# A transformer block with attention to a context and routed experts: another order for the cross stage, and element 0's cross queries split and sent by GpSimd

## The reference

```python
xn = ada_ln(x, t_emb, ...)                      # layer norm, scale and shift from the condition
x = x + mha(xn, xn, xn, sa ...)                 # self attention: 16 heads of 8, 512 keys
x = x + mha(x, u, u, ca ...)                    # cross attention to the 77 context rows
xn = ada_ln(x, t_emb, ln2 ...)
x = x + gelu(xn @ ffn_w1 + b1) @ ffn_w2 + b2    # 128 -> 512 -> 128
# second layer
nx = layer_norm(x)
evidence = softmax(nx @ Wq @ (ctx @ Wk).T * 128**-0.5) @ (ctx @ Wv)
combined = [nx, evidence, condition]            # 384 wide
router_probs = softmax(combined @ router_W + router_b)            # 3 experts
routed = sum_e(expert_e(combined) * router_probs[e])              # silu MLPs, 384 -> 256 -> 128
g = sigmoid(silu(combined @ gate_w1 + b) @ gate_w2 + b)
out = x + g * (routed @ out_w + out_b)
```

## Time and profile before

| | |
|---|---|
| median of 3 runs | 282.58 us (280.73 to 287.5) |
| the profiled execution | 281.71 us, span 279.9 us |
| mean granted TensorE clock | 0.933 |
| busy: TensorE, VectorE, ScalarE, GpSimd | 230.6, 160.4, 156.4, 48.1 us |
| self attention, from first score to last | about 40 to 149 us |
| cross attention of both elements, with the first feed-forward | about 149 to 213 us |
| the rest | about 213 to 280 us |

### The profile page before, as it was taken

The page is one execution under the profiler, slowest core; times in us unless marked ns, Lnnn a source line. Parts: engine busy times, 40 slices in busy tenths (PEclk is TensorE's granted clock), DMA queues, the critical chain, the costliest instruction groups (busy, mean ns, idle before and its releaser), DMA issues.

```text
span 279.9 us, 3963 instructions
## 1 busy us (share of the span) xinstructions
PE 230.6 (82%) x1304; PEld 98.9 (35%) x1304; DVE 160.4 (57%) x377; ACT 156.4 (56%) x280; POOL 48.1 (17%) x124
## 2 busy tenths in 40 slices
PE   3489799896989888789887878659968999968982
PEld 2123243351224222222332214323224555553752
DVE  6979755776588895979630135760035481353543
...
PEclk9999955998699999799999978995999999999999
...
GB/s 237 402 116 219 36 134 128 10 122 99 35 3 1 4 0 3 148 79 2 5 6 4 0 0 2 2 2 5 1 0 1 2 1 0 0 2 37 0 0 37
DMA packets 7012, 13.20 MB, mean 47 GB/s; under 512 B 1746, under 2 KB 5394, under 8 KB 6578
## 3 DMA queue, kind: packets, MB, share of 16 engines
...
## 4 chain that ended last, share of the span: by engine, by line
PE 62%; DVE 17%; ACT 8%; issue 4%; DMA 3%; POOL 3%; SPq 1%; DVEq 0%; POOLq 0%; ACTq 0%
PE UP L755 8%; PE S L703 7%; DVE negm L1214 5%; PE ST L729 4%; PE ST L959 3%; PE S L910 3%; ACT PT L1041 3%; PE UP L758 3%; PE ST L954 2%; ACT mT L1084 2%; PE MB L860 2%; PE ST L978 2%; DMA xn<-x_nat 2%; PE ST L732 2%; PE S L915 1%
## 5 line engine op out<-in xcount | busy, mean ns | idle before, releaser
L1041 ACT ACTIVATE PT<-ST 128x512 f32<-128x512 f32 (+1 forms) x160 | 84.2, 592 | 21.1 <-PE ST L729 13.8
L1214 DVE TENSOR_REDUCE negm<-S 128x1 f32<-128x512 f32 x128 | 80.0, 682 | 27.5 <-PE S L703 27.2
L729 PE MATMUL ST<-QS,KS 51*128 51x512 bf16 x128 | 42.2, 412 | 5.6 <-ACT PT L1041 5.3
L703 PE MATMUL S<-KS,QS 48*128 48x512 bf16 x128 | 42.0, 418 | 3.2 <-DVE negm L1214 2.3
L755 PE MATMUL UP<-PT,VS 128*32 128x512 f32 x256 | 37.3, 657 | 0.0
L703 PEld LDWEIGHTS S<-KS,QS 48*128 48x128 bf16 x128 | 10.1, 97 | 36.8 <-issue 33.7
L577 POOL CAST mpart<-negm 128x16 bf16<-128x16 f32 x16 | 3.2, 199 | 113.6 <-DVE negm L1214 71.6
L1084 ACT COPY mT<-MB 12x512 bf16<-12x512 bf16 x16 | 9.2, 573 | 16.6 <-PE MB L860 16.6
L1218 DVE TENSOR_REDUCE negm<-S 128x4 f32<-128x308 f32 x32 | 13.5, 471 | 5.7 <-PE S L709 5.7
L729 PEld LDWEIGHTS ST<-QS,KS 51*128 51x128 bf16 x128 | 10.7, 96 | 15.0 <-issue 10.7
L624 POOL TENSOR_TENSOR rstd<-rstd,half 128x4 f32<-128x4 f32 x4 | 4.1, 1018 | 55.0 <-DVE rstd L1266 55.0
...
## 6 DMA issues: line engine op xcount, KB each, us to landing
...
```

What stands on the lines that cost most here:

```text
L703: last = mm(S[:, n % 3, :], QS[r, b, 2 * g + jj, i * P:(i + 1) * P], KS[r, b, 2 * g + jj, :], start=True, stop=True)
L729: mm(ST[:, k % 3, :], KS[r, b, block, kt * P:(kt + 1) * P], QS[r, b, block, :], start=True, stop=True).then_inc(s["st_ready"], 1)
L1041: a(PT[0:rows, n % 2, j, :], ST[0:rows, k % 3, :], ACT.Exp, scale=SCALE).then_inc(s["exp_out"], 1)
L1214: v.tensor_reduce(negm[:, slot, e // 4, e % 2, e // 2 % 2:e // 2 % 2 + 1], S[:, n % 3, :], AX.X, ALU.max, negate=True).then_inc(s["max_out ...
```

## The change

The list of steps is reordered in four places, and the resources follow.

- Start: `early_q` stands ahead of the first `mrows`. In each round with `mrows` one `maxima` now comes between `values` and `mrows`. `small_router` moves from round 5 to round 7, `strips_x` from 7 to 8.
- After self attention: `turn`, `project`, `residual`, `queries` stand earlier in the rounds. For element 0 ScalarE writes the cross queries once in fp32 (`rest`), GpSimd makes the three parts, and issues `stack` and, four rounds later as a step `strips_q`, `strips`; before, SP issued them and VectorE made two of the parts. Element 1 keeps ScalarE and VectorE.
- Cross stage: written out in full. All blocks go through ring S; ScalarE copies blocks 3, 5 and 7, VectorE the others. Scores and exponentials of element 1 begin before the last maxima; element 0's norm runs beside them; all exponentials of element 1 come before the first gelu of element 0.
- Tail: the norm and the feed-forward of element 1 stand earlier, among the context attention of element 0. The first norms use UP, MB and S[2]; some banks of the experts change places.

```diff
@@ -145,6 +146,7 @@
             steps.append(fill.pop(0))
     maxima(2)
     maxima(2)
+    steps.append(later.pop(0))
     steps.append(("mrows",) + units[0])
     for n in range(LEAD - 2):
...
     put(3, 0, ("strips1",))
-    for n, step in ((3, "small_ln"), (4, "small_hidden"), (5, "small_router")):
+    for n, step in ((3, "small_ln"), (4, "small_hidden"), (7, "small_router")):
         put(n, len(ROUND) - 1, (step,))
-    put(7, 0, ("strips_x",))
+    put(8, 0, ("strips_x",))
     for n in range(3):
         put(11 + n, len(ROUND) - 1, ("fold", n))
     for n, (unit, kt) in enumerate(rounds):
...
         if unit == (CROSS, 1, 0):
-
-            steps.append(("values",) + rounds[n - 1] + (n - 1,))
-            chain = [step for where in sorted(due) for step in due[where] if step[0] != "reach"]
-            due.clear()
-            gather, natural, normalise, turn, project, residual = chain
-
-            def group_maxima():
-
...
-            put(n + 2, 0, ("norm", 1, 0))
-            put(n + 3, len(ROUND) - 1, ("norm_back", 1, 0))
+            break
         if kind == SELF and kt == 2 and units[at + 1][0] == SELF:
-            put(n, WITH_V + 1, ("mrows",) + units[at + 1])
+            put(n, WITH_V + 2, ("mrows",) + units[at + 1])
         if unit == (SELF, 1, GROUPS - 1):
-            put(n, WITH_V + 1, ("mrows", CROSS, 0, kt))
+            put(n, WITH_V + 2, ("mrows", CROSS, 0, kt))
         if last and g % 2 == 1:
             r = g // 2
             put(n + 1, WITH_V + 1, ("gather", kind, b, r))
-            put(n + 2, 0, ("natural", kind, b, r))
-            put(n + 2, 1, ("normalise", kind, b, r))
+            put(n + 2, 0 if kind == SELF else WITH_V + 1, ("natural", kind, b, r))
+            put(n + 2, 1 if kind == SELF else WITH_V + 2, ("normalise", kind, b, r))
             if r == 1:
-                put(n + 2, WITH_V + 2, ("turn", kind, b))
-                put(n + 3, WITH_V - 1, ("project", kind, b))
-                put(n + 3, WITH_V, ("residual", kind, b))
-                if kind == SELF:
-                    put(n + 3, len(ROUND) - 1, ("queries", b))
-                    put(n + 4, 1, ("rests", b))
-                    put(n + 5, len(ROUND) - 1, ("reach", (3 + b) * GROUPS))
+                put(n + 2, WITH_V, ("turn", kind, b))
+                put(n + 2, len(ROUND) - 1, ("project", kind, b))
+                put(n + 2, len(ROUND) - 1, ("residual", kind, b))
+                put(n + 3, WITH_V - 1, ("queries", b))
+                put(n + 3, WITH_V + 1, ("rests", b))
+                if b == 0:
+                    put(n + 7, len(ROUND) - 1, ("strips_q",))
+                    put(n + 5, len(ROUND) - 1, ("reach", 3 * GROUPS))
+                else:
+                    put(n + 4, WITH_V, ("xblock", 0))
+                    put(n + 4, WITH_V, ("xblock", 1))
         for place, token in enumerate(ROUND):
             for step in due.pop((n, place), []):
...
+            elif token != "V":
                 steps.append(("scores", unit, kt, n, token))
                 steps.append(("exps", unit, kt, n, token))
-    steps += [("values",) + rounds[-1] + (len(rounds) - 1,), ("gather", CROSS, 1, 1)]
...
+    def cross_maxima(g):
+
+        for _ in range(EVENTS[CROSS]):
+            maxima(len(units))
+
+    def attend(n, *js):
+
+        for j in js:
+            steps.append(("scores", rounds[n][0], 0, n, j))
+            steps.append(("exps", rounds[n][0], 0, n, j))
+
+    def values(n):
+        steps.append(("values",) + rounds[n] + (n,))
+
+    n = len(rounds) - GROUPS
+    cross_maxima(0)
+    steps += [("xblock", 2), ("xblock", 3), ("mrows", CROSS, 1, 0)]
+    values(n - 1)
+    steps += [("gather", CROSS, 0, 1)]
+    cross_maxima(1)
+    steps += [("xblock", 4), ("natural", CROSS, 0, 1), ("normalise", CROSS, 0, 1), ("xblock", 5), ("mrows", CROSS, 1, 1)]
+    cross_maxima(2)
+    steps += [("turn", CROSS, 0), ("xblock", 6), ("xblock", 7)]
+    attend(n, 0, 1, 2)
+    steps += [("mrows", CROSS, 1, 2), ("project", CROSS, 0), ("residual", CROSS, 0)]
+    cross_maxima(3)
+    attend(n, 3)
+    steps += [("norm", 0, 0)]
+    attend(n + 1, 0, 1, 2)
+    steps += [("mrows", CROSS, 1, 3)]
+    attend(n + 1, 3)
+    values(n)
+    attend(n + 2, 0, 1, 2)
+    values(n + 1)
+    steps += [("gather", CROSS, 1, 0), ("norm_back", 0, 0)]
+    attend(n + 2, 3)
+    attend(n + 3, 0, 1, 2)
+    steps += [("natural", CROSS, 1, 0), ("normalise", CROSS, 1, 0)]
+    attend(n + 3, 3)
+    steps += [("ffn1", 0, 0), ("ffn1", 0, 1)]
+    values(n + 2)
+    steps += [("ffn1", 0, 2)]
+    values(n + 3)
+    steps += [("gather", CROSS, 1, 1), ("ffn1", 0, 3), ("natural", CROSS, 1, 1), ("normalise", CROSS, 1, 1)]
+    steps += [("ffn2", 0, 0), ("ffn2", 0, 1)]
+    steps += [("ffn2", 0, 2), ("ffn2", 0, 3), ("turn", CROSS, 1), ("norm", 1, 0), ("project", CROSS, 1), ("residual", CROSS, 1)]
+    steps += [("norm", 0, 1), ("norm_back", 1, 0), ("context", 0), ("hidden_x", 0, 0), ("norm_back", 0, 1), ("hidden_x", 0, 1)]
+    steps += [("ffn1", 1, 0), ("context_probs", 0), ("ffn1", 1, 1), ("ffn1", 1, 2), ("context_value", 0), ("ffn1", 1, 3)]
     steps += [("hidden_ev", 0, 0), ("router", 0), ("hidden_ev", 0, 1)]
-    steps += hidden(0, 2, 3)
-    steps += [("norm_back", 0, 1), ("router_probs", 0)]
-    steps += hidden(0, 3, 4) + [("gate", 0)]
-    steps += [("ffn1", 1, c) for c in range(NF)]
...
-    steps += [("ffn2", 1, c) for c in range(NF)]
-    steps += hidden(0, 5, 6) + [("tanh", 0), ("norm", 1, 1)] + hidden(0, 6, 7)
-    steps += [("expert", 0, 1), ("norm_back", 1, 1), ("expert", 0, 2), ("context", 1), ("out", 0)]
-    steps += [("hidden_x", 1, c) for c in range(3)] + [("context_probs", 1)]
-    steps += [("hidden_x", 1, 3), ("context_value", 1), ("hidden_x", 1, 4), ("hidden_x", 1, 5)]
+    steps += hidden(0, 2, 3) + [("ffn2", 1, c) for c in range(NF)] + [("router_probs", 0)]
+    steps += hidden(0, 3, 4) + [("norm", 1, 1), ("gate", 0)]
+    steps += hidden(0, 4, 5) + [("expert", 0, 0)] + hidden(0, 5, 6) + [("norm_back", 1, 1), ("tanh", 0)]
+    steps += hidden(0, 6, 7) + [("context", 1), ("expert", 0, 1), ("hidden_x", 1, 0), ("context_probs", 1)]
+    steps += [("expert", 0, 2), ("out", 0), ("hidden_x", 1, 1), ("context_value", 1)]
+    steps += [("hidden_x", 1, c) for c in range(2, 5)]
     steps += [("hidden_ev", 1, 0), ("router", 1), ("hidden_ev", 1, 1), ("hidden_ev", 1, 2), ("router_probs", 1)]
-    steps += [("gate", 1), ("hidden_ev", 1, 3), ("expert", 1, 0), ("hidden_ev", 1, 4), ("tanh", 1), ("hidden_x", 1, 6)]
+    steps += [("gate", 1), ("hidden_ev", 1, 3), ("expert", 1, 0), ("hidden_x", 1, 5), ("hidden_ev", 1, 4), ("tanh", 1), ("hidden_x", 1, 6)]
     steps += [("hidden_ev", 1, 5), ("expert", 1, 1), ("hidden_ev", 1, 6), ("expert", 1, 2), ("out", 1)]
...
-            return S[:, i, :] if (site, b) == (1, 0) else bank(b, i)
+            return S[:, i, :] if (site, b) == (1, 0) else bank(b, i) if site else (UP[:, :], MB[:, :])[i] if b else S[:, 2, :]
...
-            return [bank(1, 0), bank(1, 1), bank(0, 2), bank(0, 3), bank(0, 0), bank(0, 1)][c % HIDDEN_RING[1]]
+            return [bank(1, 0), bank(1, 1), bank(0, 3), bank(0, 0), bank(0, 1), bank(0, 2)][c % HIDDEN_RING[1]]
         def expert_bank(b, e):
...
                                      ).then_inc(s[f"mrows_in{n % 2}"], 16)
-                elif step == ("queries", 0):
-                    stack(sp, scr_q[B], part[:, 0, :, :], Q_RUNS, s["stack_qx0"],
-                          [(x, 1) for x in ("qx1_out", "qx2_out", "qx3_out")])
-                    sp.wait_ge(s["stack_qx0"], STACK_DMAS)
...
+                elif step == ("queries", 0):
+                    pool.wait_ge(s["qxf_out"], 1)
+                    parts_of(rest[:, 0, :], part[:, 0, :, :], s["split_qx"], 0)
+                    stack(g, scr_q[B], part[:, 0, :, :], Q_RUNS, s["stack_qx0"], [("split_qx", x) for x in (1, 3, 4)])
+                elif step[0] == "strips_q":
+                    pool.wait_ge(s["stack_qx0"], STACK_DMAS)
+                    strips(g, QX[:, 0, :, :], scr_q[B], s["strips_qx0"])
...
-                    if k % 2:
-                        n = event_at[step]
-                        pe.wait_ge(s["max_out"], n - 2)
-                        dst, done = S[:, n % 3, :], "s_ready"
-                    else:
-                        dst, done = (ST[:, 2, :], UP[:, :])[k // 2 % 2], "xblock_ready"
-                        if k == 0:
-                            pe.wait_ge(s["exp_out"], HEADS * CROSS_1)
-                        elif k == 2:
-                            pe.wait_ge(s["u_out"], 3 * B)
-                        else:
-                            pe.wait_ge(s["xblock_act"], k // 2 - 1)
+                    n = event_at[step]
+                    pe.wait_ge(s[reader_of[n - 3][0]], reader_of[n - 3][1])
                     for p, out in enumerate(("qx1_out", "qx2_out", "qx3_out")):
                         if k == 0:
-                            pe.wait_ge(s[out], B)
```

(30 more changed lines are left out.)

70 lines of the change are left out of this document (26 added, 44 removed).

## The result

The changed kernel takes **287.56 us** in the median of four executions (286.42 to 294.12), the kernel before 282.44 (280.73 to 287.5). The ratio is 1.019, with a 95% interval of 1.011 to 1.026: slower by 1 to 2.6%. The forecast was 270.7, in a range of 262.5 to 279; it was wrong by 17 us and in its sign. The profiled execution took 287.06 us.

A forecast was written before the change was run, and what follows sets the result against it. TensorE (busy 82%) was taken as the bound, its waits costing themselves plus half-clock stretches behind. 4.3 + 3.3 + 1.1 + 3.2 + 0 = 11.9 us off 281.7 gave 269.8, plus 0.9 for the median 270.7; range 262.5 to 279.

The forecast's parts named there:

- the layout: Cross stage and tail, new order laid out by hand: 19.1 us idle against 18.1, 5.0 us ahead at full clock throughout.
- its clock term: Cross stage and tail: half-clock time behind two groups of new gaps, costing 2.0 and 3.0 us.
- "0": Cross stage and tail: net gain taken as 0 us, with ends +5.0 and −4.0.
- "a stretch of 6.8 us behind each" group: Cross stage: 6.8 us at half clock behind each of two groups of waits, 3.7 and 4.2 us in 5.
- The slower rival: Tail: gaps near 205, 232 and 244 each start a 13.4 us half-clock stretch, whole kernel 285.7 us; chance 0.08.
- the 34 from which on it was to decide the sign: Behind 149 us: slow time past about 34 us would make the kernel slower, against 13.6 before.
- Queries of element 0: Cross queries made on GpSimd: the 1.56 us wait and 1.75 us of half-clock cost go; gain 3.3 us.
- "SP's queue loses all of it, so its maxima rows are only freer": Element 0's query transfers move from SP's to GpSimd's queue, so SP's maxima rows could only gain; no size given.
- Router 4.3: Self attention, small products two rounds later: 1.9 us of wait and 2.4 us of half-clock cost go, 4.3 us.
- rows 1.1: Self attention, one maxima product ahead of each maxima row fills half of 2.3 us waiting for GpSimd: 1.1 us.
- early queries 3.2: Start, early query product ahead of the first maxima row: fills most of 1.35 us, halves a half-clock stretch; 3.2 us.
- "about 0.3": Self attention, TensorE's 2.23 us wait for GpSimd's split of unit 2 shrinks to about 0.3 us, gaining 1.9 us.

The follow-up runs named there:

- the three edits alone (second run): Kernel before with only the router's small products later, early query product first and maxima rows one product later: 286.94 us over twelve executions, ratio 1.011.

## Why the prediction was wrong

**Cross stage and tail: the layout was right, its clock term was mis-sized.** The waits came where and nearly as long as forecast. At equal half-clock time the part is level: 138.5 − 0.344 × 36 = 126.1 us, before 130.7 − 0.344 × 13 = 126.2; "0" was right but for the clock. The term that failed is "a stretch of 6.8 us behind each" group: they were 17 and 13.6 us. I priced unseen gaps by the median stretch of the trace, though the same rows held one of 13.4 us. The slower rival came near in size and not in place: it had 40 us behind the gaps near 205, 232 and 244, and measured were 36, none of it behind the last two and half of it behind the first group. That 36 lies just above the 34 from which on it was to decide the sign is chance, for that sum took the self attention's gain as kept. Its price of half a microsecond for each was too high: 0.344. And part of the 7.8 us is the mild trace that the forecast started from; some 3.3 are the change's.

**Queries of element 0: gain 3.3, measured none.** VectorE's three parts and the wait of 1.56 us went, as forecast. The step that failed is "SP's queue loses all of it, so its maxima rows are only freer". The rows got slower, 6.21 us instead of 1.9, with the transfer issued from GpSimd's queue 1.17 us ahead of them. TensorE then waited 4.35 us, and 6.5 us at half clock followed. The strips took 7.1 us, not the 3.7 of the earlier trace rows, which were for half the bytes; I had watched whether they came in time, not who was in flight with them.

**Router 4.3, rows 1.1, early queries 3.2: the waits went, the time did not.** The waits for GpSimd's split fell from 5.5 to 0.9 us up to the first cross maxima, and the first self attention score came at 36.94 (forecast 37). Two steps failed. One is that the wait of 2.23 us becomes "about 0.3" for the end as well. What I left out is what is late next: the maxima rows of the same unit land only when element 1's strips have drained, at 63.5 to 73.0 us. In eleven of the eighteen traces with this edit TensorE waits 1.17 to 3.86 us for them, in two 0.20 (the changed kernel's is one), and in five not at all, where it comes late itself. (In the changed kernel the waits for rows rose from none to 4.5 us, but 4.35 of that are the queries'.)

The other is the stretch of the earlier trace rows behind the first wait, of which half (3.2 us) was booked as gained. In the changed kernel's trace it is gone. In that of the three edits alone (second run), the wait is just as short and the stretch is back, 13.7 us at half clock:

```profile
32.79 0.59 PE L861 MATMUL MB<-ident,mpart 128*12 128x128 bf16 x4 [0.30 <-POOL mpart L584]
```

```profile
32.50:46.50 14.00, 13.01 (x47) 5.12 (x47) 7.75 (x13) 7.02 (x14) 8.70 (x13) 0.51 0.36 122
```

Of the seventeen traces with the wait of 0.30 us, four have 13.7 us there, five 3.4 and eight none; of the three with 1.35 us, two have 13.7 and one 6.8. So the wait makes the stretch likelier, but it comes without it too; what else decides it, no run shows. At an equal clock the three edits cost 0.3 ± 1 us over 16 executions, for 8.6 forecast. In the changed kernel the first part is 3.5 us shorter, which is about the 11.5 us less at half clock (4.0 by the slope).

**The step from one profile to the median.** The stretches ahead of 149 us were read from one execution as belonging to three waits. The kernel before has 27 to 65 us of half-clock time from one execution to the next, 0.344 us each: 13 us that no edit explains. The trace had 37.5, the mean is 46.8. Edits worth 2 us can't be read off a single span.
